# A weight fold moved from VectorE to 128 small fp32 products on TensorE, with GpSimd's transfers behind the first tap

## What is computed

```
x                                        # (8, 64, 128, 64): batch, channel c, time, v
xp = pad(x, time, 8 more, mode="edge")
patches = xp[:, :, 8 * n + p, :]         # n = 0..15 patches, p = 0..15 samples
xf = rfft(patches over p, norm="ortho")  # 9 frequencies, real and imaginary
h = concat(real, imag) @ W.T             # W: (64, 1152) = (o, 18 frequency parts x 64 channels)
h = layernorm(h + attention(h))          # 16 * 64 * 8 = 8192 tokens of 64 numbers
h = layernorm(h + experts(h))
```

## Time and profile before

| | us |
|---|---|
| median of three runs | 940.5 |
| the profiled execution | 937.71 |
| its span, first to last instruction | 935.9 |
| PE busy in the span | 878.7 |
| VectorE busy | 765.4 |
| ScalarE busy | 650.2 |
| GpSimd busy | 145.8 |

### The profile page before, as it was taken

One profiled execution on the slowest core, in us unless ns is written; L12 is line 12 of the kernel. 1 busy time (PEld: TensorE's weight loads), 2 busy tenths in 40 slices (PEclk: granted clock), 3 DMA queues, 4 the chain that ended last, 5 costly groups with the idle time before them and its releaser, 6 DMA issues.

```text
span 935.9 us, 30575 instructions
## 1 busy us (share of the span) xinstructions
PE 878.7 (94%) x13276; PEld 438.7 (47%) x13276; DVE 765.4 (82%) x919; ACT 650.2 (69%) x1260; POOL 145.8 (16%) x153
## 2 busy tenths in 40 slices
PE   3998899999999999999999999999999799888885
PEld 2443455555555555555555555555555454333321
DVE  5134988998999899989999988998898788676663
ACT  0134788887888788788887887888787686655543
POOL 3045500000000040000000000000000948432122
PEclk9999999999999999999999999999999999899898
DMA  9797500000000000000000000000000000001001
GB/s 253 197 290 127 98 2 3 2 3 2 2 2 3 3 2 3 2 2 2 3 3 2 3 3 2 3 2 3 2 3 3 2 2 2 1 12 23 12 12 34
DMA packets 28709, 26.52 MB, mean 28 GB/s; under 512 B 9536, under 2 KB 26176, under 8 KB 28576
## 3 DMA queue, kind: packets, MB, share of 16 engines
q1 hardware_dynamic: 19408, 14.98, 7.0%
q10 hardware_dynamic: 8752, 8.93, 3.7%
q0 software_dynamic: 416, 0.66, 0.4%
HBM read 18.28 MB, written 2.10 MB: 22 GB/s over the span
## 4 chain that ended last, share of the span: by engine, by line
PE 84%; DVE 4%; POOL 4%; ACT 3%; DMA 2%; issue 2%; SPq 0%; POOLq 0%; ACTq 0%; DVEq 0%
PE ps L442 33%; PE ps L459 23%; PE ps L472 11%; PE ps L375 6%; PE ps L528 3%; DMA ring<-in_x_dram 2%; PE ps L593 2%; PE ps L485 2%; DVE ring L1003 1%; PE ps L609 1%; ACT ring L772 1%; DVE ring L872 1%; PE ps L506 1%; ACT ring L739 1%; POOL stat L297 1%
## 5 line engine op out<-in xcount | busy, mean ns | idle before, releaser
L872 DVE TENSOR_TENSOR ring<-ring 128x1024 f16<-128x1024 f32 x512 | 602.4, 1225 | 52.2 <-ACT ring L772 50.6
L772 ACT ACTIVATE ring<-ps 128x1024 f32<-128x1024 f32 x512 | 519.3, 1020 | 131.2 <-PE ps L442 130.9
L442 PE MATMUL ps<-big 64*64 64x512 f16 x6144 | 376.8, 377 | 9.4 <-ACT ring L772 9.2
L459 PE MATMUL ps<-ring,fs 64*64 64x512 bf16 x4096 | 274.6, 384 | 0.0
L442 PEld LDWEIGHTS ps<-big 64*64 64x64 f16 x6144 | 171.3, 106 | 173.9 <-ACT ring L772 15.1
L459 PEld LDWEIGHTS ps<-ring,fs 64*64 64x64 f16 x4096 | 116.0, 106 | 110.4 <-issue 0.5
L472 PE MATMUL ps<-ring,fs 64*64 64x512 f16 x2048 | 154.0, 377 | 0.1
L772 ACT ACTIVATION_READ_ACCUMULATOR ring<-ps 128x1 f32 x512 | 101.3, 198 | 0.0
L472 PEld LDWEIGHTS ps<-ring,fs 64*64 64x64 f16 x2048 | 58.5, 107 | 53.5 <-issue 1.2
L739 ACT ACTIVATE ring<-ps,b1s 128x512 f32<-128x512 f32 x64 | 42.1, 683 | 46.8 <-PE ps L528 46.8
L1003 DVE TENSOR_TENSOR ring<-ring,ps 128x512 f32<-128x512 f32 x64 | 43.4, 683 | 33.4 <-ACT ring L739 30.8
(11 more groups left out here) (135 smaller groups left out, 434.9 us busy)
## 6 DMA issues: line engine op xcount, KB each, us to landing
ring<-in_x_dram ACTq DMA_DIRECT2D x8, 1024.0 KB, 15.6
ring<-in_x_dram SPq DMA_DIRECT2D x8, 1024.0 KB, 13.2
big<-big SPq DMA_DIRECT2D x16, 128.0 KB, 2.4
out_dram<-h SPq DMA_DIRECT2D x16, 128.0 KB, 2.4
f<-in_L_tok_W_dram SPq DMA_DIRECT2D x1, 288.0 KB, 4.1
xedge<-in_x_dram POOLq DMA_DIRECT2D x2, 128.0 KB, 9.0
w1s<-in_L_ffn_w_dram POOLq DMA_DIRECT2D x2, 128.0 KB, 8.3
fs<-consts_dram ACTq DMA_DIRECT2D x1, 256.0 KB, 18.8
```

What stands on the lines that cost most here:

```text
L442: last = mm(bank(SLOT_BANK[slot_of(s)] + r)[m:m + 64, :], of_k[r][:, 128 * k + m:128 * k + m + 64], of_q[r][:, q0 + 512 * r:q0 + 512 * r + ...
L459: last = mm(bank(sums_bank(s // NT) + half)[m:m + 64, :], fs[64 * r:64 * r + 64, s % NT, m:m + 64], probs[64 * r:64 * r + 64, s % 8, :].bi ...
L772: a(probs[:, s % 8, :], bank(SLOT_BANK[slot_of(s)], 2), ACT.Exp, accum_out=rowsum[:, s:s + 1]).then_inc(s_pr, 1)
L872: tt(probs_lo[:, s % 8, :], probs[:, s % 8, :], probs[:, s % 8, :].bitcast(BF16)[:, 1:2 * QC:2], ALU.subtract).then_inc(s_lo, 1)
```

## The change

W is loaded otherwise: four transfers of 16 outputs each, group k on the partitions 32k to 32k + 17, the 18 frequency parts on partitions, outputs and channels behind. The coefficients in `cst` are laid out to fit: on the same partitions, 8 columns for the first half of a stride and 8 for the second (tap and sample block). PE then makes the taps itself: for each of 16 outputs j, each group k and each half one product, 18 rows deep, with 64 channels of W as weights and 8 coefficient columns streamed, 128 in all. Each writes 64 partitions x 8 columns of PSUM, bank 4 + k. VectorE only copies from PSUM to `weff`, two copies of 128 x 64 for each tap. GpSimd waits for the first tap (`s_weff` >= 1) before it issues its first load.

```diff
         @block.sync
         def _(sp):
-            sp.dma_start(wraw, W.rearrange("o (g c) -> o g c", c=C)).then_inc(s_wg, 16)
+            for k in range(4):
+                sp.dma_start(wg[32 * k:32 * k + NF], W[OB * k:OB * k + OB].rearrange("o (g c) -> g o c", c=C)).then_inc(s_wg, 16)
...
             pool.wait_ge(s_zero, 3)
+            pool.wait_ge(s_weff, 1)
             for half in range(2):
...
             pe.wait_ge(s_cst, 16)
-            pe.wait_ge(s_wg, 16)
-            for g in range(NF):
-                for rows in (0, 64):
-                    last = mm(ps[rows:rows + 64, 2048 + D * g:2048 + D * g + D], wraw[:, g, :], ident[0:D, 0:D],
-                              start=True, stop=True)
+            pe.wait_ge(s_wg, 64)
+            for j in range(OB):
+                for k in range(4):
+                    for half in range(2):
+                        last = mm(bank(4 + k)[64 * half:64 * half + 64, TAPS * j:TAPS * j + TAPS], wg[32 * k:32 * k + NF, j, :],
+                                  dft[32 * k:32 * k + NF, TAPS * half:TAPS * half + TAPS], start=True, stop=True)
             last.then_inc(s_wfold, 1)
...
             for s in range(HALF):
-                taps = dft[:, s, :].rearrange("p (r f) -> p r f", r=2).unsqueeze(3).to_broadcast([128, 2, FH, D])
-                w, v = wdft[s % 2], wsum[s % 2]
-                folded(tt(w, raw, taps, ALU.mult), 5 * s + 1)
-                folded(tt(v[:, 0:FH], w[:, 0], w[:, 1], ALU.add), 5 * s + 2)
-                folded(tt(v[:, FH:FH + 4], v[:, 0:4], v[:, 4:8], ALU.add), 5 * s + 3)
-                folded(tt(v[:, 0:2], v[:, FH:FH + 2], v[:, FH + 2:FH + 4], ALU.add), 5 * s + 4)
-                folded(tt(v[:, 2], v[:, 0], v[:, 8], ALU.add), 5 * s + 5)
-                tt(weff[:, s, 0:D], v[:, 2], v[:, 1], ALU.add)
-                tt(weff[:, s, D:2 * D], v[:, 2], v[:, 1], ALU.subtract).then_inc(s_weff, 1)
+                for a in range(2):
+                    last = cp(weff[:, s, D * a:D * a + D].rearrange("p (k o) -> p k o", k=4), folded[:, s, a])
+                last.then_inc(s_weff, 1)
```

More of the change, by code:

```diff
@@ L21 @@
 NF = 2 * (PATCH // 2 + 1)
-FH = NF // 2
 D = 64
@@ L25 @@
 HALF = STRIDE // 2
+OB = D // 4
+TAPS = 2 * HALF
 BP = B // 2
@@ L71 @@
 XLEN = NM * HALF * V
-CONSTS = 128 + HALF * NF + E + D + 1 + G
+CONSTS = 128 + 2 * TAPS + E + D + 1 + G
 LATE_CONSTS = 128 + MASKS + 128
@@ L81, in constants @@
         for s in range(HALF):
[L82 to L86, removed]
+            for part in range(2):
+                for f in range(NF // 2):
+                    a = 2 * math.pi * f * (STRIDE * part + HALF * half + s) / PATCH
+                    for k in range(4):
+                        col = 128 + TAPS * half + 2 * s + part
+                        c[32 * k + f, col] = math.cos(a) / math.sqrt(PATCH)
+                        c[32 * k + NF // 2 + f, col] = -math.sin(a) / math.sqrt(PATCH)
+    at = 128 + 2 * TAPS
     c[:, at:at + E] = np.arange(E) - E
@@ L122, in tower @@
         ident = cst[:, 0:128]
-        dft = cst[:, 128:128 + HALF * NF].rearrange("p (s g) -> p s g", s=HALF)
-        at = 128 + HALF * NF
+        dft = cst[:, 128:128 + 2 * TAPS]
+        at = 128 + 2 * TAPS
         enum = cst[:, at:at + E]
@@ L148, in tower @@
         f = sb("f", [128, NT, D], F32)
-        wraw = f[0:D, 0:NF, :]
-        wdft = [h[:, NF * i:NF * i + NF, :].rearrange("p (r f) o -> p r f o", r=2) for i in range(2)]
-        wsum = [h[:, 2 * NF + 14 * i:2 * NF + 14 * i + 14, :] for i in range(2)]
+        wg = f[:, 0:OB, :]
         fs = sb("fs", [128, NT, 2 * D], F16)
@@ L199, in tower @@
         s_id16, s_zero, s_b2r, s_b2c, s_b2 = (sem(n) for n in ("s_id16", "s_zero", "s_b2r", "s_b2c", "s_b2"))
-        s_wfold, s_weff, s_fold, s_sqf, s_wpad = (sem(n) for n in ("s_wfold", "s_weff", "s_fold", "s_sqf", "s_wpad"))
+        s_wfold, s_weff, s_sqf, s_wpad = (sem(n) for n in ("s_wfold", "s_weff", "s_sqf", "s_wpad"))
         s_prod, s_prodev, s_tr, s_h, s_pad, s_padev = (sem(n) for n in ("s_prod", "s_prodev", "s_tr", "s_h", "s_pad", "s_padev"))
@@ L813, in _ @@
             dve.wait_ge(s_wfold, 1)
[L814 to L818, removed]
+            folded = ps[:, 2048:].rearrange("p (k n) -> p k n", k=4)[:, :, 0:OB * TAPS].rearrange("p k (o s a) -> p s a k o", s=HALF, a=2)
             for s in range(HALF):
-                taps = dft[:, s, :].rearrange("p (r f) -> p r f", r=2).unsqueeze(3).to_broadcast([128, 2, FH, D])
-                w, v = wdft[s % 2], wsum[s % 2]
-                folded(tt(w, raw, taps, ALU.mult), 5 * s + 1)
-                folded(tt(v[:, 0:FH], w[:, 0], w[:, 1], ALU.add), 5 * s + 2)
-                folded(tt(v[:, FH:FH + 4], v[:, 0:4], v[:, 4:8], ALU.add), 5 * s + 3)
-                folded(tt(v[:, 0:2], v[:, FH:FH + 2], v[:, FH + 2:FH + 4], ALU.add), 5 * s + 4)
-                folded(tt(v[:, 2], v[:, 0], v[:, 8], ALU.add), 5 * s + 5)
-                tt(weff[:, s, 0:D], v[:, 2], v[:, 1], ALU.add)
-                tt(weff[:, s, D:2 * D], v[:, 2], v[:, 1], ALU.subtract).then_inc(s_weff, 1)
+                for a in range(2):
+                    last = cp(weff[:, s, D * a:D * a + D].rearrange("p (k o) -> p k o", k=4), folded[:, s, a])
+                last.then_inc(s_weff, 1)
             dve.wait_ge(s_weff, HALF)
```

## The result

| | median, us | range, us | runs | against before, 95% interval |
|---|---|---|---|---|
| before | 940.6 | 938.0 to 941.7 | 8 | |
| after | 945.2 | 943.1 to 946.4 | 8 | 1.0053 (1.0041 to 1.0064) |

The kernel became slower by 4.6 us, where the forecast was 2.5 us faster and the range ended at 945.0. The profiled execution of after took 946.19 us, with a span of 944.4 us: 8.5 us more than the profiled one of before. One execution is not the median: of these 8.5 us, 7.2 lie ahead of the mark (the start of the edge product) and 1.3 behind it. Over the profiled executions of all kernels of this study the stretch behind the mark takes 898 to 902 us of the span, and batch 1 of x lands at 19.7 to 23.3 us in the four kernels that load W and x as before does and only hold GpSimd's transfers back. So steps are read from traces, the size of the effect from medians.

The account below looks back on a forecast made before the run. It took x's transfer, batch 1 landing at 23.9 us, to bound the first stage. First tap 19.9 + products 13.7 + clock 1.4 + GpSimd's packets 0.4 = 35.4 us against 37.94: -2.5 us, so 938.0 us, range 934.5 to 945.0.

Parts of the forecast that it names:

- Where the bound lies: First stage: x's transfer comes last, the fold is hidden; the end moves by what the edge product's start (37.94 us) moves.
- W's landing: W's four loads, 1152 small packets on SP's queue: landed at 10.0 us, with 6.7 and 14 as ends.
- the sign of being wrong: The prediction is wrong if PE's first record comes after 12 us; the first new product was expected near 10 us.
- x behind W: Batch 1 of x on SP's queue: 19.7 us without q0, W's small packets add 1.9 less 0.8 us, landing at 20.8.
- The fold's pace: The new fold on PE, 256 records at 36 ns each: 9.2 us, ends 8.5 us (33 ns) and 14.1 us (55 ns).
- The rival of a slow fold at 55 ns: PE's strips do not overlap in the fold, 55 ns a record make 14.1 us: 942.9 us; chance 0.17.
- Taps: VectorE's eight PSUM copies: two give the first tap in 0.4 us, at 19.9 us; the other six, 1.2 us, are hidden.
- First products: PE's 32 records behind the first tap: 13.7 us plus 1.4 us for half clock, no wait for batch 1, ending at 35.0.
- PE comes from the fold without a gap: PE enters the first products straight from the fold; 1.4 us counted for half clock, between 0 and 2.0.
- GpSimd's wait: GpSimd's queue (q0) costs x 4.2 us; kept quiet until the first tap, batch 1 would land at 19.7 instead of 23.9.
- `b2raw`: GpSimd's delayed load lands at about 35.4 us, wanted at 35.9, a tie; 0.4 us counted for it and batch 3 together.
- W late from uneven engines: Only nine of sixteen engines carry W's packets, 128 rounds, W lands at 14.2 us: 942.2 us; chance 0.17.

Follow-up runs that it names:

- ScalarE's x out of the way: The changed kernel, in which ScalarE issues its halves of x only when W has landed; 948.3 us, 1.0088 of before.
- The run without small packets: Before with GpSimd waiting for the first tap, and SP issuing its first x only after GpSimd's three memsets; 941.55 us, 1.0018 of before.
- the run with GpSimd's wait alone: Before with one line added: GpSimd waits for the first tap before its first load; 935.88 us, 0.9953 of before.
- 16 rows: The changed kernel with W's loads and products cut from 18 to 16 rows, two frequency parts left out; one run, 944.01 us.

## Why the prediction was wrong, step by step

The steps below follow the profiled executions, in which the mark came 9.8 us and the end 11.0 us after the forecast (45.16 for 35.4, 946.19 for 935.2). The median is 7.2 us above it (945.2 for 938.0), since before was profiled 2.8 us below its median and after 1.0 above.

**Where the bound lies: right.** What lies behind the mark moves with it, to within the 4 us by which that stretch varies; x, not the fold, held the first products, before and after.

**W's landing: wrong.** I took 10.0 us; it was 15.5, beyond even my upper end of 14 and beyond the 12 us that I had named as the sign of being wrong. The step that failed is "small packets of another queue were served in turn with x's, one for one" from the first byte on. It was read from 9 to 12 us of before, where all queues were long under way. At the start there is no such turn: SP's queue, whose second to fourth load of W and whose x were issued after ScalarE's x, moved 41 packets from 5 to 8 us, with half of W among what it held. With ScalarE's x out of the way W landed at 6.1 us. The run without small packets shows the same standstill from a delay of 0.48 us. Why a later issue stands is open; that it does is what the forecast lacked. A second part is the spread: I let all the engines finish together, but W's 1152 packets had gone by count at 12.1 us and the last landed 3.4 us later. The packets themselves, which I had counted as the danger, pass at about 500 a microsecond when the queue is alone.

**x behind W: wrong, and this decides.** I added 1.9 - 0.8 us for W's packets to the 19.7 us of a batch 1 without q0: 20.8. It was 29.9. Two terms failed. The first is the same standstill: SP's first issue of x moved from 1.36 to 2.55 us behind the four issues of W (0.31 to 0.54 us each), which I had counted for W's landing and forgotten for x. The second is the price of a small packet: I took 27 ns of an engine each, but while the queues share, a 256 B packet of W takes a turn that would have carried 1 KB of x.

The bytes on q1 give their sizes, as an estimate, against the run with GpSimd's wait alone (batch 1 at 20.2 us). By 9 us q1 had moved 0.17 MB instead of 0.90, which at the 0.17 MB a microsecond of a sharing queue is about 4.2 us; by 15 us it was 0.62 instead of 1.94, another 3.4 us, and by 18 us no more. The last 2 us are a slower pace from 22 us on (110 to 143 packets a microsecond until 27 us) and later stragglers. I had 1.1 us for all of it.

**The fold's pace: mis-sized on both sides.** 36 ns a record was 14.4 ns, so 9.2 us became 3.7 with an even pace. Below even my lower end of 33, which came from L410 with twice as many weight columns. The Trainium skill's floor of about 25 ns between small matmuls (TensorE: Matmul & The Clock Gate, back-to-back issue gap) stood nearer, and these records still ran below it; why, no run shows. But a pause of 4.5 us came on top, which no row of before showed: 8.4 us from the first record to the last. That this is near the 9.2 us of the forecast is luck, two errors that nearly cancel. The rival of a slow fold at 55 ns fell.

**Taps: right.** The first tap is at 24.4 us, 0.5 us behind the fold's last record at 23.92 (0.3 + 0.4 us forecast), and the eight copies, 1.14 us in all, are hidden.

**First products.** 24.38 + 3.78 + 1.78 of waiting + 15.22 = 45.16, against 19.9 + 13.7 + 1.4 = 35.0. Of the 10.2 us, 4.5 are the later tap, 1.8 the wait for batch 1 and 3.9 the clock: 3.78 us for four records that need 1.72 at 2.4 GHz, and 3.2 us too much for the 28, 5.3 us in all, where I had 1.4 for both. My remark that PE comes from the fold without a gap held for neither: the fold itself rested PE for 4.5 us, and batch 1 was late.

**GpSimd's wait: right in size.** 4.2 us forecast for x's landing, 3.7 us in the trace and 4.1 in the medians where the wait stands alone. In after it is worth 2.7 us of x's landing and nothing at the mark. `b2raw` cost nothing (L427 follows L423 directly at 46.02 us), and batch 3 showed no new wait over 0.2 us.

**The rivals.** That of W late from uneven engines (942.2) named the right place and direction, and its 14.2 us came near the 15.5. Its mechanism, rounds of packets on nine engines, is not shown: stragglers there were, but with 16 rows as well, and the standstill it did not have. None of the rivals had x late on its own account; with x on time, the tap's 4.5 us alone would have given an estimated 942.5.

## What to carry to other kernels

When two queues carry halves of the same data, compare the times of their first large issues, not only the bytes: half a microsecond more on one of them cost 5.7 us here, a collision that followed from it included, and more and smaller pieces ahead of a queue's main load are paid there. Read a queue's rate where it starts, not only where it runs. A wait that holds transfers off a critical load can be the best line of a larger change, so it pays to run each half alone.

## What the runs showed of the hardware that I had not expected

- **One queue of the two stands still.** The queue whose x was issued later moved 40 packets in 3 us (5 to 8 us, SP late), 41 (after), or none from 6.1 to 13 us (ScalarE late). In each case the other ran alone at 170 to 190 packets of 1 KB a microsecond with the engines' time full (104 to 112%), where two together move 340. The Trainium skill (DMA: Bandwidth & Descriptors, issuing engines are not separate DMA queues) says that transfers of different issuing engines run on the same 16 engines and interleave; from 9 to 12 us in the earlier trace rows they do, at the start they don't. What holds the later queue isn't settled, and the gap between the issues alone doesn't tell how long it stands.
- **Small packets and large ones take turns alike.** From 10 to 15 us of after q1 moved 620 packets with 0.39 MB and q10 621 with 0.63 MB: in this shared stretch a piece of 256 B took a turn like one of 1 KB.
- **Code loading pauses PE.** 223 records of small products outrun PE's instructions: a stop of 1.2 us with idle DMA engines, 4.5 us beside x, 7.2 us in the worst case, and in all seven kernels the work went on 2.3 to 2.7 us behind one packet of the instruction queue.
- **Small fp32 products on changing strips** of 18 rows, 64 weight columns and 8 streamed ran at 14.4 ns a record.
- **The granted clock and the pace.** From 29 to 35 us of after the granted clock reads 1.00 in the view by stretches (columns as in the earlier trace rows), while the weight loads stand 0.85 us apart, twice the 0.43 us of later; in before, from 25 to 29 us, the same distance went with 0.58:

```profile
31.00:33.00 2.00, 2.00 (x4) 0.95 (x3) 0.00 (x0) 0.00 (x0) 2.00 (x5) 1.00 1.10 167
```

  Over so short a stretch the distance of equal records tells the level better than the clock column.
